# A two-layer gated transformer block on one core: the seam between keys/values and attention, and the last gate-and-up block of a pair, rearranged

## What is computed

```python
q = rms_norm(x_ln @ wq, q_norm_w); k = rms_norm(x_ln @ wk, k_norm_w); v = x_ln @ wv
k_ctx = rms_norm(ctx @ wk_ctx, k_norm_w); v_ctx = ctx @ wv_ctx
q, k = rope(q), rope(k)                       # 16 query heads, 4 heads of keys and values, of 128
probs = softmax(q @ [k_ctx, k].T / sqrt(128) + causal mask on the own keys)
x = x + tanh(g_xattn[0]) * (probs @ [v_ctx, v]) @ wo
n = layernorm(x)
h = silu(n @ w_gate) * (n @ w_up)             # inner width 2048
h = keep, of every 4 neighbours, the 2 largest by size
x = x + tanh(g_ffn[0]) * h @ w_down
```

## Time and profile before

| | us |
|---|---|
| median of three runs | 2112.15 |
| lowest, highest | 2109.58, 2112.73 |
| the profiled execution | 2108.11 |
| its span on the core | 2106.3 |
| TensorE busy (share of the span) | 1942.6 (92%) |
| VectorE busy | 1350.0 (64%) |
| ScalarE busy | 1079.6 (51%) |
| mean granted TensorE clock, of full | 0.968 |

### The profile page before, as it was taken

One profiled execution on the slowest core, in us unless ns is written; L12 is line 12 of the kernel. 1 busy time (PEld: TensorE's weight loads), 2 busy tenths in 40 slices (PEclk: granted clock), 3 DMA queues, 4 the chain that ended last, 5 costly groups with the idle time before them and its releaser, 6 DMA issues. The chain is left out here.

```text
span 2106.3 us, 30642 instructions
## 1 busy us (share of the span) xinstructions
PE 1942.6 (92%) x10514; PEld 1486.9 (71%) x10514; DVE 1350.0 (64%) x2408; ACT 1079.6 (51%) x2590; POOL 431.5 (20%) x515
## 2 busy tenths in 40 slices
PE   6999789999999999969999999999979978886898
PEld 5888667777777777757887778778768855553444
DVE  6777577777777777744424655554745438885886
ACT  4333266666766666652314321121324329994998
POOL 1111144444444444410000000000000002222111
PEclk9999899999999999989999999999999989997999
DMA  6776853333332330146433221223287422331121
GB/s 251 262 261 218 297 155 110 82 91 91 101 89 83 100 80 23 31 137 228 145 100 130 60 60 40 61 61 107 94 294 247 149 82 96 116 101 51 33 59 45
DMA packets 209028, 253.76 MB, mean 120 GB/s; under 512 B 12246, under 2 KB 158822, under 8 KB 202476
## 3 DMA queue, kind: packets, MB, share of 16 engines
q1 hardware_dynamic: 208876, 251.82, 37.2%
HBM read 151.10 MB, written 100.68 MB: 120 GB/s over the span
## 5 line engine op out<-in xcount | busy, mean ns | idle before, releaser
L971 ACT ACTIVATE at_prob<-at_S,at_bias,at_rq 128x384 f32<-128x384 f32 (+1 forms) x256 | 185.2, 733 | 131.5 <-DVE at_bias L1058 124.3
L1069 DVE TENSOR_TENSOR at_pt_lo<-at_PT,at_pt_hi 128x512 fp32r<-128x512 f32 x224 | 154.8, 692 | 84.6 <-ACT at_pt_hi L978 84.6
L835 POOL TENSOR_SCALAR at_prob<-at_prob,at_rsum 128x384 f32<-128x384 f32 (+1 forms) x256 | 161.4, 643 | 148.9 <-DVE at_rsum L1064 148.8
L1722 ACT ACTIVATE gu_silu<-gu_G 128x512 f32<-128x512 f32 x64 | 38.1, 597 | 242.7 <-PE gu_G L103 233.0
L1049 DVE TENSOR_REDUCE at_nmax<-at_S 128x1 f32<-128x384 f32 (+1 forms) x256 | 152.7, 619 | 6.6 <-PE at_S L885 2.3
L978 ACT ACTIVATE at_pt_hi<-at_PT 128x512 fp32r<-128x512 f32 x224 | 134.9, 603 | 42.3 <-PE at_PT L892 42.3
L1759 DVE TENSOR_TENSOR gu_h<-gu_silu,gu_U 128x512 f32<-128x512 f32 x64 | 43.9, 688 | 150.9 <-PE gu_U L103 104.0
L892 PE MATMUL at_PT<-c_ident,at_prob 128*128 128x128 f32 x896 | 126.0, 275 | 3.5 <-DVE at_pt_lo L1069 3.5
L824 POOL TENSOR_TENSOR at_q<-at_by_cos,at_by_sin 128x512 f32<-128x512 f32 x64 | 82.4, 1288 | 215.3 <-DVE at_qv L1044 183.3
L881 PE MATMUL at_S<-at_k_hi,at_q_hi 128*128 128x384 f32 (+1 forms) x256 | 109.7, 428 | 7.5 <-DVE at_q_lo L1074 7.5
L892 PEld LDWEIGHTS at_PT<-c_ident,at_prob 128*128 128x128 f32 x896 | 100.3, 140 | 22.4 <-DVE at_pt_lo L1069 14.2
(11 more groups left out here) (341 smaller groups left out, 5470.8 us busy)
## 6 DMA issues: line engine op xcount, KB each, us to landing
wide<-at_ot SPq DMA_DIRECT2D x64, 256.0 KB, 2.9
wide<-gu_h SPq DMA_DIRECT2D x64, 256.0 KB, 3.3
o_a<-wide SPq DMA_DIRECT2D x14, 1024.0 KB, 4.8
d_a<-wide SPq DMA_DIRECT2D x13, 1024.0 KB, 8.6
keys_hi<-kv_kt_hi SPq DMA_DIRECT2D x16, 512.0 KB, 3.2
keys_lo<-kv_kt_lo SPq DMA_DIRECT2D x16, 512.0 KB, 4.2
values_hi<-kv_v_hi SPq DMA_DIRECT2D x16, 512.0 KB, 4.8
values_lo<-kv_v_lo SPq DMA_DIRECT2D x16, 512.0 KB, 5.1
```

The lines of the kernel that those rows point to most:

```text
L835: pool.tensor_scalar(prob[u % 2][:, h, 0:n], prob[u % 2][:, h, 0:n], rsum[:, s:s + 1], 1.0, ALU.mult, ALU.mult).then_inc(normed.sem, 1)
L971: act.activation(prob[u % 2][:, h, 0:n], S[h][:, 0:n], ACT.Exp, bias=bias[:, s:s + 1], scale=rq[u % 4][:, h:h + 1], accum_out=sums[:, s:s ...
L1069: dve.tensor_tensor(pt_lo[f % 4][:], bank_of("p", u, kb)[:], pt_hi[f % 4][:].bitcast(F32), ALU.subtract).then_inc(pt_done.sem, 1)
```

## The change

Two edits that have nothing to do with each other.

**The seam.** The tiles with the last keys and values (`kt_hi`, `kt_lo`, `v_hi`, `v_lo` of the tokens) now come from the room that lives on into the attention, which uses the same tiles as `prob` and `pt_hi`, `pt_lo`. The last four stores raise a semaphore of their own, `kv_last`, and the first stage no longer waits for them; the attention's SyncE waits for them before it loads `wq` over the tiles. The split of the first `wq` piece moves from behind the last pair into its sixth tile, the idle transposes are halved, and the attention raises `xt_arrived` ahead of its small loads.

**Gate and up.** In the last block of a pair but the last pair, TensorE takes G and U in turn for each piece of the tokens and says after each piece that it is free (`n_free`); ScalarE and VectorE split the next pair's tokens before they turn to the last block's silu and product.

```diff
@@ keys_values, SyncE, the stores of two tiles @@
+                    stored = kv_stored[s].sem if more or n < NT else c.kv_last
...
-            for s in (xt_stored, ct_stored, *kv_stored):
+            for s in (xt_stored, ct_stored, kv_stored[1]):
                 sp.wait_ge(s.sem, s.per * (PAIRS + 1))
+            sp.wait_ge(*kv_stored[0].at(PAIRS - 1, 64))
...
-            keep_awake(pe, T[0], c, 2 * AWAKE)
+            keep_awake(pe, T[0], c, AWAKE)
...
+                    if not more and i == TT + 1:
+                        split_queries_hi(0)
                 keep_keys(turn, NT - 1)
...
+                    if not more and i == TT + 1:
+                        split_queries_lo(0)
                     if more and i == 2:
@@ attention, tiles and SyncE @@
-        prob = [mem.sb(f"prob{i}", [P, GROUP, 2 * L]) for i in range(2)]
+        prob = [c.kt_hi, c.kt_lo]
...
+            for b in range(2):
+                sp.sem_inc(xt_arrived[b].sem, 32)
             sp.dma_start(cosw[:], io["c_cos_tok"]).then_inc(setup, 16)
...
-            for b in range(2):
-                sp.sem_inc(xt_arrived[b].sem, 32)
             load_kv(0, 0, 0)
+
+            sp.wait_ge(c.kv_last, 4 * 16)
             for n in range(HKV - AHEAD):
                 weights.load(sp, n)
@@ gate_up, TensorE @@
+            def last_block(turn):
+
+                i = IC - 1
+                q, j = divmod(i, 4)
+                pe.wait_ge(w_ready, 2 * q + 2)
+                pe.wait_ge(*silu_done.at(turn, i - 1))
+                pe.wait_ge(*h_done.at(turn, i - 1))
+                for k in range(DC):
+                    for n, bank, full in (("g", G[i % 2], G_full), ("u", U[i % 2], U_full)):
+                        last = three_passes(pe, bank[:], [(w_hi[n][q][:, k, j, :], w_lo[n][q][:, k, j, :],
+                                                           n_hi[:, k, :], n_lo[:, k, :])],
+                                            start=(k == 0), stop=(k == DC - 1))
+                        if k == DC - 1:
+                            last.then_inc(full.sem, 1)
+                        elif n == "u":
+                            last.then_inc(n_free.sem, 1)
...
                     if more and i == IC - 1:
                         turn_xn(turn + 1)
+                        last_block(turn)
+                        continue
@@ gate_up, ScalarE; on VectorE split_n moves in the same way ahead of product(turn, i) @@
             def split_n(turn):
-                act.wait_ge(*U_full.at(turn, 0))
                 for n in range(DC):
+                    act.wait_ge(*(n_free.at(turn - 1, n + 1) if n < DC - 1 else U_full.at(turn, 0)))
...
                 for i in range(IC):
+                    if more and i == IC - 1:
+                        split_n(turn + 1)
...
-                if more:
-                    split_n(turn + 1)
                 sizes(turn, NC - 1)
```

More of the change, by code:

```diff
@@ L273, in keys_values @@
         names = ["L0_xattn_wk_ctx", "L0_xattn_wv_ctx", "L0_xattn_wk", "L0_xattn_wv"]
-        kt_hi = [mem.sb(f"kt_hi{s}", [P, HKV, TOK]) for s in range(SRC)]
-        kt_lo = [mem.sb(f"kt_lo{s}", [P, HKV, TOK]) for s in range(SRC)]
+        kt_hi = [c.kt_hi, mem.sb("kt_hi1", [P, HKV, TOK])]
+        kt_lo = [c.kt_lo, mem.sb("kt_lo1", [P, HKV, TOK])]
         weights = WeightSplit(mem, [(io[n].rearrange("(k p) n -> p k n", p=P), whole, w_hi[i][:], w_lo[i][:])
@@ L289, in keys_values @@
         kn = [mem.sb(f"kn{i}", [P, 512]) for i in range(2)]
-        v_hi = [mem.sb(f"v_hi{s}", [P, TT, HKV * HD], F32R) for s in range(SRC)]
-        v_lo = [mem.sb(f"v_lo{s}", [P, TT, HKV * HD], F32R) for s in range(SRC)]
+        v_hi = [c.v_hi, mem.sb("v_hi1", [P, TT, HKV * HD], F32R)]
+        v_lo = [c.v_lo, mem.sb("v_lo1", [P, TT, HKV * HD], F32R)]
         cosw = mem.sb("cosw", [P, 2, HD])
@@ L390, in body @@
                     tok, tiles = slice((t - 1) * P, (t + 1) * P), slice(t - 1, t + 1)
+                    stored = kv_stored[s].sem if more or n < NT else c.kv_last
                     wait_apart(sp, kt_done, turn, n, passed)
                     for dram, keys in ((scr.k_hi, kt_hi), (scr.k_lo, kt_lo)):
-                        sp.dma_start(dram[turn, s, :, :, tok], keys[s][:, :, tok]).then_inc(kv_stored[s].sem, 16)
+                        sp.dma_start(dram[turn, s, :, :, tok], keys[s][:, :, tok]).then_inc(stored, 16)
                     wait_apart(sp, v_done, turn, n, passed)
@@ L513, in keep_keys, with split_queries_hi @@
                                ACT.Copy).then_inc(kt_hi_done.sem, 1)
+            def split_queries_hi(i):
+                act.wait_ge(wq_arrived[i], 16)
+                act.wait_ge(*V_full.at(PAIRS - 1, TT))
+                act.activation(c.wq_hi[i][:], (x, cx)[i][:], ACT.Copy).then_inc(wq_hi_done, 1)
             def body(turn, more):
@@ L541, in _ @@
             turns(act, body)
-            for i in range(2):
-                act.wait_ge(wq_arrived[i], 16)
-                act.wait_ge(*V_full.at(PAIRS - 1, TT))
-                act.activation(c.wq_hi[i][:], (x, cx)[i][:], ACT.Copy).then_inc(wq_hi_done, 1)
+            split_queries_hi(1)
         @block.vector
@@ L557, in split_keys, with split_queries_lo @@
                                   kt_hi[s][:, :, own], ALU.subtract).then_inc(kt_done.sem, 1)
+            def split_queries_lo(i):
+                dve.wait_ge(wq_hi_done, i + 1)
+                dve.tensor_tensor(c.wq_lo[i][:], (x, cx)[i][:], c.wq_hi[i][:].bitcast(F32),
+                                  ALU.subtract).then_inc(wq_lo_done, 1)
             def split_lo(turn, n):
@@ L629, in _ @@
             turns(dve, body)
-            for i in range(2):
-                dve.wait_ge(wq_hi_done, i + 1)
-                dve.tensor_tensor(c.wq_lo[i][:], (x, cx)[i][:], c.wq_hi[i][:].bitcast(F32),
-                                  ALU.subtract).then_inc(wq_lo_done, 1)
+            split_queries_lo(1)
 def attention(nc, io, c, scr):
@@ L670, in attention @@
         rsum = mem.sb("rsum", [P, S_N])
-        prob = [mem.sb(f"prob{i}", [P, GROUP, 2 * L]) for i in range(2)]
+        prob = [c.kt_hi, c.kt_lo]
         weights = WeightSplit(mem, [(wq[:, :, g * GW:(g + 1) * GW], whole, wq_hi[g][:], wq_lo[g][:])
                                     for g in range(AHEAD, HKV)], raw=prob)
-        pt_hi = [mem.sb(f"pt_hi{i}", [P, GROUP * P], F32R) for i in range(4)]
-        pt_lo = [mem.sb(f"pt_lo{i}", [P, GROUP * P], F32R) for i in range(4)]
+        pt_hi = [c.v_hi[:, i, :] for i in range(4)]
+        pt_lo = [c.v_lo[:, i, :] for i in range(4)]
         ot = [mem.sb(f"ot{i}", [P, GROUP, L]) for i in range(2)]
@@ L1663, in _ @@
         def _(pe):
-            for s in (T_full, G_full, U_full):
+            for s in (T_full, G_full, U_full, n_free):
                 s.start(pe)
@@ L2626, in make_queries, with far @@
         self.queries = ExitStack()
-        def far(name, shape):
-            return self.queries.enter_context(nc.sbuf_tensor("queries_" + name, shape, F32R, side="right"))
+        def far(name, shape, dt=F32R):
+            return self.queries.enter_context(nc.sbuf_tensor("queries_" + name, shape, dt, side="right"))
         self.wq_hi = [far(f"wq_hi{i}", [P, DC, 512]) for i in range(2)]
         self.wq_lo = [far(f"wq_lo{i}", [P, DC, 512]) for i in range(2)]
+        self.kt_hi, self.kt_lo = (far(f"kt_{part}", [P, HKV, TOK], F32) for part in ("hi", "lo"))
+        self.v_hi, self.v_lo = (far(f"v_{part}", [P, TT, HKV * HD]) for part in ("hi", "lo"))
+        self.kv_last = nc.alloc_semaphore("queries_kv_last")
         self.xt_hi = far("xt_hi", [P, DC, TOK])
```

10 lines of the change are left out of this document (6 added, 4 removed).

## The result

| | before | after |
|---|---|---|
| median | 2111.39 us (4 runs, 2109.58 to 2112.73) | 2085.95 us (4 runs, 2083.89 to 2087.91) |
| ratio, 95% interval | | 0.988 [0.9863, 0.9897] |
| the profiled execution | 2108.11 | 2086.45 |
| its span | 2106.3 | 2084.6 |
| mean granted TensorE clock | 0.968 | 0.974 |

The kernel is 1.2% faster: 25.4 us between the medians, 21.7 between the two profiled executions. 2087.7 was forecast, within 2082.0 to 2093.0. Four single executions among the runs further down, which took from 2499 to 9261 us, are in none of the medians and ratios.

What follows compares the result with a forecast made beforehand. TensorE, busy 92% of the span, was taken as the bound. Gains of 17.8 us in gate and up and 6.7 between first stage and attention, 24.5 together, took the median 2112.15 to 2087.7 us, range 2082.0 to 2093.0.

Steps and rivals of the forecast that it cites:

- The seam: Between first stage and attention: without the store wait and with an earlier signal, TensorE starts 6.7 us earlier.
- The holes close: Gate and up's three changes of pair: TensorE's idle hole of 4.04 us each, 12.1 in all, goes entirely.
- The low clock goes: First pass behind each change of pair: low-clock excess of 1.68, 2.40 and 2.53 us, 6.6 together, goes.
- The third rival: At the changes of pair the low clock stays though the hole goes; 6.6 us not returned, 2094.3 us; chance 0.06.
- The new wait: Third block after each change of pair: TensorE waits 0.2 to 0.3 us for VectorE's later product, 0.9 in all.
- The slower rival: VectorE becomes the bound at the changes of pair, late by 7.4 us at each: 2116.4 us or more; chance 0.02.
- Gate and up in all: Gate-and-up stage: 18.7 us from holes and low clock, less 0.9 of new wait, net gain 17.8 us.
- The tables: Attention's opening: tables for rotating the first queries are made by 248.1 us, wanted at 248.8, so covered by 0.7.
- The first rival: Attention's opening: small loads behind stores take 8.4 us, tables come late, rotation waits 4.2: 2091.8 us; chance 0.09.
- the sum: Whole kernel: 17.8 us from gate and up plus 6.7 from between first stage and attention, 24.5 us gained.

## Why the prediction was right

**The holes close.** Forecast 3 x 4.04 = 12.1 us and no hole left; the steps across all three changes are 0.23 us. The pieces come as worked out: the high halves 1.36 us apart, each low half 0.63 behind its high half's start, the last one done at 1218.20, where the next pair wants it at 1216.68 + 9 x 0.227 = 1218.72. That is a margin of 0.5 us, as forecast.

**The low clock goes.** Forecast 6.6 us. The granted clock is 1.00 behind every change; the kernel with the holes filled gives the price by itself, 6.4. The third rival falls with it.

**The new wait.** Forecast 0.2 to 0.3 us in the third block, 0.9 in all. It is there, at that place, for VectorE's product: 0.17, 0.16 and 0.16 us idle at 1230.61, 1319.84 and 1409.08. By steps, as the holes were measured, it is 0.33 each (0.56 from start to start instead of 0.23), so 1.0 in all. The profile after has the wait for gu_h five times, 5.7 us; the other two, 4.5 and 0.7, stood in the kernel before with 4.9 and 0.5. The slower rival, which lives on this wait, needed 7.4 us.

**Gate and up in all.** Forecast 17.8. Between the first block's start and the last block's the kernel after is 17.6 us shorter (362.9 for 380.5), the one with these edits alone 18.2.

**The seam.** Forecast 6.7, measured 6.66 at TensorE's start. The steps: the first split starts at 223.85 (forecast 223.95) and takes 2.29; the last one ends at 239.69 (forecast 240.0; the 0.3 us that were to be left over did not appear, the last kt_lo starts at 235.60 as forecast without them); SyncE's last issue ends at 240.06 (forecast 240.3); the first load goes out 2.1 behind it, where I had 1.9. The gap behind the waking transposes is 4.7 (forecast 4.5), and the clock is low in the first seven of the first pass's twelve matmuls; the forecast had the pass as slow as before, where ten were slow.

**The tables.** Landing forecast 3.5 us after the issue at about 243.6; it was 3.8. The four small loads behind the stores took 3.1 to 3.8 us against 2.7 for the mask before. The first rival, with 8.4, falls. But the cover of 0.7 us was not there: the squares ended at 247.99 and the tables, with the mask made behind them, at 248.36, so the rotation came 0.4 us late. I had put the place where they are wanted 6.5 us behind TensorE's start as before; the first pass ran its last five matmuls at full clock this time and was over sooner. The Trainium skill, DMA: Bandwidth & Descriptors, section Queues, rings and completion order, has a small load stand behind every store issued before it. The trace does not contradict that: the last store landed at 244.4 and the four loads between 245.3 and 247.4, all of them behind it. When the first of them was issued, at 242.19, that store had 2.2 us to go, so there was little to stand behind.

**Where the sum was off.** In the profiled executions 21.7 us came for 24.5. The 2.8 are: 1.0 lost of the seam's 6.7 by the start of gate and up (the attention's first S is 7.5 ahead; by 293 it is 6.2 and stays so to the last one, and in between the granted clock was 0.63 in the window 266 to 280 that is shown with the idle matmuls, where the kernel before had 0.76 in 273 to 287); 0.2 in gate and up; 1.1 in the wait at the seam to the down projection (11.8 for 10.7), which varies by more than this between kernels that do not touch it; 0.5 behind it. No term of the sum failed; the tables' 0.4 us, put at nothing, were paid for by the first pass, whose squares were done 0.8 sooner than counted. I had counted no place where the gain is given back, and the low-clock stretches and that wait move by a microsecond or two from one execution to the next. The unedited kernel's second profiled execution had a span of 2080.2 us, where 2081.8 was forecast and 2084.6 came first. The median of 2085.95 is 1.7 under the forecast of 2087.7: between the medians the change gave 25.4, and the kernel before came out at 2111.39 with a fourth run. The mechanism is borne out place by place; that the medians came within 1.7 us of the forecast is in part luck, with runs of one kernel 3 to 4 us apart.

## What to carry over

Where one engine's wait for a handful of small steps comes round at each turn of a loop, look first at their order on the engine that makes them: putting them ahead of work that is wanted later gave 3.5 to 4.3 us a turn here, and setting the producer free piece by piece the last 1.8. A hole costs its own length and, when the clock falls in it, the excess of the pass behind it; read both from the timeline (4.0 and 1.7 to 2.5 us here), and price idle matmuls by their passes, for they only pay while they end before the wait does. An explicit wait for stores at the end of a stage can go when the next stage leaves their tiles alone: the landing (3.7 us) goes under the next stage's opening, but a gain at the start of a long program has to be compared in pairs at its end, where 2 to 4 us of it are no more than what executions of one kernel differ by.

## What was not expected of the hardware

- **Idle matmuls of float type.** One matmul of 128 columns of the plain float type is two records and takes 0.23 us (7.31 us for 32, 9.99 for 44), in every place where it was tried: as long as the step of one matmul of 512 columns of the rounded type.
- **Short holes and the clock.** At full clock, idle gaps of 1.5 us (between blocks) and 1.89 us (at the seam) had full-clock steps behind them; after 2.65 us the first six matmuls started at steps of 0.22 to 0.31 and the next ones at 0.43; after 3.9 and 4.7 between six and all twelve matmuls of the pass behind stepped at 0.41 or more. These are a few places, most read off one execution each.
- **The end of a stage.** From the last instruction of the latest engine to the next stage's first it took 1.9 us with TensorE as the latest engine, 1.9 to 2.1 from the last store's landing to the first load before, with the signal moved and with the wait put back, and 2.1 in the changed kernel.
